# A two-layer LSTM kernel: an own semaphore for the clearing of c, and the two waits of the cell scan written in the other order

## What is computed

```python
def step(carry, xp_t):
    prev_h, prev_c = carry
    h_bar = xp_t + prev_h @ Wh
    i = jax.nn.sigmoid(h_bar[:, 0:Hdim])
    f = jax.nn.sigmoid(h_bar[:, Hdim:2 * Hdim])
    o = jax.nn.sigmoid(h_bar[:, 2 * Hdim:3 * Hdim])
    g = jnp.tanh(h_bar[:, 3 * Hdim:4 * Hdim])
    next_c = f * prev_c + i * g
    next_h = o * jnp.tanh(next_c)
    return ((next_h, next_c), next_h)
```

## Time and profile before

| What | Value |
|---|---|
| median of 3 runs | 485.77 us (484.74 to 487.51) |
| the profiled execution | 481.0 us |
| span of the profiled execution, first to last instruction | 479.0 us |
| mean granted TensorE clock | 0.996 of 2.4 GHz |
| busy: TensorE matmul, VectorE, ScalarE | 97%, 54%, 44% |

### The profile page before, as it was taken

The page is one execution under the profiler, slowest core; times in us unless marked ns, Lnnn a source line. Parts: engine busy times, 40 slices in busy tenths (PEclk is TensorE's granted clock), DMA queues, the critical chain, the costliest instruction groups (busy, mean ns, idle before and its releaser), DMA issues.

```text
span 479.0 us, 17186 instructions
## 1 busy us (share of the span) xinstructions
PE 462.4 (97%) x6440; PEld 349.3 (73%) x6440; DVE 260.7 (54%) x1422; ACT 212.1 (44%) x1092; POOL 17.4 (4%) x29
## 2 busy tenths in 40 slices
PE   7999999999999999999999999999999999999997
PEld 5777666777666777766789877777777777777775
DVE  4545555555555555555545655555555555555554
ACT  2444444544444445444435344444444444444443
POOL 6700000000000000000000000000000000000000
PEclk9989999999999999999999999999999999999999
DMA  5010111110011111010000000000000000000000
GB/s 163 8 19 2 15 16 16 16 16 12 5 16 16 16 16 16 2 15 11 11 13 3 7 19 19 16 16 16 8 8 16 16 16 16 15 1 16 16 16 11
DMA packets 11689, 8.12 MB, mean 17 GB/s; under 512 B 1097, under 2 KB 11129, under 8 KB 11674
## 3 DMA queue, kind: packets, MB, share of 16 engines
q1 hardware_dynamic: 10874, 6.17, 6.5%
q0 software_dynamic: 512, 1.22, 0.9%
q10 hardware_dynamic: 288, 0.52, 0.3%
HBM read 2.87 MB, written 1.05 MB: 8 GB/s over the span
## 4 chain that ended last, share of the span: by engine, by line
PE 88%; DVE 4%; ACT 3%; issue 3%; DMA 1%; DVEq 0%; ACTq 0%
PE fobank L387 20%; PE gibank L377 16%; PE fobank L377 13%; PE bankV L363 5%; PE gibank L352 4%; PE bankY L531 4%; PE gibank L357 4%; PE fobank L352 4%; PE bankU L524 3%; PE fobank L357 3%; DVE cell L750 2%; PE bankV L441 2%; ACT scan L665 2%; PE bankU L459 2%; PE bankU L363 2%
## 5 line engine op out<-in xcount | busy, mean ns | idle before, releaser
L387 PEld LDWEIGHTS fobank<-ring,whf 128*128 128x128 f32 x510 | 76.5, 188 | 94.7 <-DVE ring L753 94.6
L662 ACT ACTIVATE fgate<-fobank 128x16 f32<-128x16 f32 x256 | 46.9, 183 | 164.8 <-PE fobank L387 162.5
L387 PE MATMUL fobank<-ring,whf 128*128 128x16 f32 x510 | 99.5, 270 | 10.4 <-DVE ring L753 0.7
L750 DVE TENSOR_TENSOR_SCAN cell<-scan 128x48 f32<-128x48 f32 x256 | 68.8, 269 | 53.2 <-ACT scan L665 52.8
L746 DVE TENSOR_TENSOR scan<-fgate,cell 128x16 f32<-128x16 f32 x256 | 45.3, 177 | 85.6 <-ACT fgate L662 83.7
L377 PEld LDWEIGHTS gibank<-h_hi,wh_parts 128*128 128x128 bf16 x1536 | 78.8, 110 | 0.0
L753 DVE SCALAR_TENSOR_TENSOR ring<-cell,ogate 128x16 f32<-128x16 f32 x256 | 44.7, 175 | 59.9 <-ACT cell L672 59.9
L377 PE MATMUL gibank<-h_hi,wh_parts 128*128 128x16 f16 x1536 | 75.4, 169 | 0.0
L377 PE MATMUL gibank<-h_lo,wh_parts 128*128 128x16 f16 x1536 | 75.3, 169 | 0.0
L665 ACT ACTIVATE scan<-gibank 128x32 f32<-128x32 f32 x256 | 54.8, 214 | 28.2 <-PE gibank L377 0.2
L377 PE MATMUL fobank<-h_hi,wh_parts 128*128 128x16 f16 x771 | 59.9, 174 | 0.4 <-ACT fgate L662 0.4
(11 more groups left out here) (150 smaller groups left out, 467.1 us busy)
## 6 DMA issues: line engine op xcount, KB each, us to landing
rows_t<-rows SPq DMA_DIRECT2D x16, 128.0 KB
x_rows<-in_x_dram SPq DMA_DIRECT2D x17, 64.0 KB
out_dram<-y_sb SPq DMA_DIRECT2D x16, 64.0 KB
xres<-x2T SPq DMA_DIRECT2D x15, 64.0 KB, 1.9
xin<-x2T SPq DMA_DIRECT2D x14, 64.0 KB, 1.8
w<-in_L_ffn_W_dram POOLq DMA_DIRECT2D x2, 256.0 KB, 3.9
wh<-in_L_cond_Wh_dram ACTq DMA_DIRECT2D x1, 256.0 KB, 2.8
wx<-in_L_cond_Wx_dram ACTq DMA_DIRECT2D x1, 256.0 KB, 3.9
```

The lines of the kernel that those rows point to most:

```text
L387: nc.tensor.matmul(step_out(p, t, GF), whf[layer][:], ring[:, (s - 1) % STEPS, :], start=False, stop=True, skip_group_check=True).then_inc ...
L662: nc.scalar.activation(fgate[:], fobank[p][:, NB * t:NB * t + NB], ACT.Sigmoid).then_inc(f_done[layer], 1)
L750: nc.vector.tensor_tensor_scan(out=c_scan, data0=scan_mul, data1=scan_add, initial=0.0, op0=ALU.mult, op1=ALU.add).then_inc(c_ready[layer], 1)
```

## The change

The clearing of c gets a semaphore of its own, `c_cleared`, and VectorE waits for it once a layer, in `start_h`. The multiplication f*c alone now counts up `fc_done`, so the scan waits for n + 1 and no longer n + 2. And of the two waits ahead of the scan the one for the tanh (`gi_done`) is now written first, the one for f*c second. No arithmetic changes, and no instruction that computes is added or removed.

```diff
+        c_cleared = sem("c_cleared")
...
-            nc.vector.memset(c_psum, 0.0).then_inc(fc_done[layer], 1)
+            nc.vector.memset(c_psum, 0.0).then_inc(c_cleared, 1)
+            nc.vector.wait_ge(c_cleared, layer + 1)
...
                 nc.vector.tensor_tensor(out=fc_slots, in0=fgate[:], in1=c_psum,
                                         op=ALU.mult).then_inc(fc_done[layer], 1)
-                dve.wait_ge(fc_done[layer], n + 2)
                 dve.wait_ge(gi_done[layer], n1)
+                dve.wait_ge(fc_done[layer], n1)
                 nc.vector.tensor_tensor_scan(out=c_scan, data0=scan_mul, data1=scan_add, initial=0.0,
                                              op0=ALU.mult, op1=ALU.add).then_inc(c_ready[layer], 1)
```

## The result

The changed kernel takes 465.45 us (median of 4 runs, 464.69 to 466.24). The kernel before took 486.64 us in the runs beside it (484.74 to 490.51, 4 runs). The ratio is 0.9555, 95% interval 0.9492 to 0.9618: faster by 3.8 to 5.1%. In a later and larger comparison on one chip the same two kernels had medians of 481.26 us (29 runs) and 465.33 us (7 runs), which are 15.9 us apart. Their ratio is 0.9631 (0.9581 to 0.9680), and that is 15.4 to 20.2 us. Medians here are taken over all executions and ratios over those within 1.5% of the fastest of their kernel, so a ratio need not be the quotient of two medians.

What follows compares the result with a forecast made beforehand. A loop of latencies from h back to h was taken to bound the kernel. -16.2 + 0.1 (late multiplications) + 0 to 0.1 (clearing) = -16.1 us, off the median 485.77, gave 469.7 us, range 467.3 to 473.0.

Steps and rivals of the forecast that it cites:

- Which wait is the expensive one: Ahead of the scan, the wait written second becomes an instruction of its own, 21 ns in each of 256 steps.
- The price: At the scan, a carried wait costs 0.033 us, a stand-alone one 0.098; 242 steps x 0.067 = 16.2 us gained.
- The unseen price: Ahead of the scan, the stand-alone wait for VectorE's own multiplication f*c, shown by no row, was taken as 0.098 us.
- TensorE's room: Ahead of TensorE's f-gate weight load, a shortest plain pause of 0.16 us takes up starting 0.067 us earlier.
- the rivals: Nothing changes, 485.8 us (0.07); TensorE's filler limits the gain, 478.5 (0.07); slower, f*c wait last, up to 502.0 (0.06).
- The clearing of c: Its added wait on VectorE costs 0 to 0.1 us; the scan's target falling to n + 1 saves nothing itself.
- The step that failed: The whole-kernel gain of 16.1 us was taken off the runs' median 485.77, not the profiled execution's 481.0, giving 469.7 us.

Runs made afterwards that it cites:

- Run 6: The changed kernel with f*c multiplied once more into a spare tile just ahead of the real multiplication; 478.61 us, ratio 0.9869 to the kernel before.
- run 2: The kernel before with only the order of the two waits swapped, the scan still waiting for n + 2; 486.11 us, ratio 1.0073.
- run 5: The changed kernel with fc_done counted up once more per layer, so the scan waits for n + 2 again; 490.45 us, ratio 1.0141 to the kernel before.
- run 1: The kernel before, unchanged, run again; median 484.55 us over 12 executions, ratio 1.003.
- run 3: The kernel before with only the own semaphore for the clearing of c, the wait order kept; 485.96 us, ratio 1.0045.
- run 12: The changed kernel with 8 instead of 4 matmuls in the first filler; 463.62 us, ratio 0.9617 to the kernel before.
- run 11: The changed kernel, unchanged, run again; 467.13 us, ratio 0.9684 to the kernel before.

## Why the prediction was right in the change and wrong in the time

**Which wait is the expensive one: right.** The wait written second was the instruction of its own, and it lay on the chain. After the change that instruction waits for f*c and has left the chain.

**The price: right.** 0.067 us a step were forecast. The plain step went from 1.77 to 1.70 us, the two stretches that don't depend on the start give 0.069 us, and from the first to the last scan 16.3 us were saved, against 16.1 forecast.

**The unseen price: right.** The stand-alone wait for an own result was taken as 0.098 us. Run 6 measures 0.10 to 0.11.

**TensorE's room: right.** The pauses ahead of the weight load (0.39 to 0.32 us) and the overlap behind line 354 took up the 0.07 us; none of the rivals came.

**The clearing of c: wrong, without a price here.** The forecast said that the target falling from n + 2 to n + 1 "changes a register's value alone", and gave the whole gain to the order. Runs 2 and 5 show that with n + 2 the order brings nothing, since the register operation slips between the waits and takes the wait for the tanh with it. The forecast got the gain right by luck in this point, because both halves were in the change. For the order alone I had expected the whole gain (run 2), and that was wrong by 21 us (486.11 against the changed kernel's 465.33). The register operation already stood in the trace of the kernel before, on the line of the wait written first, and the prediction didn't weigh it:

```profile
L748 DVEq ALU_OP  x233: 40/40/52, 12.2 to 472.6; - x117
```

There it stood ahead of both waits and off the chain: it started 0.01 us behind the start of the multiplication (median). Between the waits, in run 2, it starts 0.03 us behind the end of the tanh and is on the chain.

**The step that failed.** It is this one: "The median of the runs, 485.77, lies 4.8 above that execution; the recurrence is the same in both, so I take the same 16.1 off." The subtraction is sound, the base was not. On the profiled execution it gives 464.9, and the changed kernel measured 465.45; but the range began at 467.3 and left the forecast's own 464.9 out. The 4.8 us were not a constant of the kernel. One program scatters between about 479 and 494 us (run 1), and the kernel before has medians of 481.26, 482.08 and 481.17 us on three chips, not 485.77. Against the larger sample the gain is 481.26 - 465.33 = 15.9 us, and the forecast's 16.1 lies within the interval of the ratio (15.4 to 20.2 us). The range was too narrow at its lower end, because it took the scatter of three runs as the scatter of the kernel: the median alone could move by the 4.8 us that stood in the table.

Where one execution loses against another is shown for profiled ones alone. All profiles of the two loops named above agree to 0.2 us within each of the two later stretches, and differ in the first 32 steps and ahead of them, while TensorE doesn't yet hold its full clock. The clock can also fall later: in run 6's profile it was 0.50 from 305 to 315 us, with 103 matmuls in these 10 us. That the first runs of the kernel before lost their 5 us at the start is inferred; they weren't profiled. It also stays open why all four of them lay above 484.7 us, where only six of the 29 later executions did. It can be chance, or something of that chip and hour.

The profiled spans differ by 14.8 us, 1.5 less than the 16.3 between the scans, and that is the start alone: the first scan started at 12.4 us in the one and at 13.9 in the other, and behind the last scan's start both have 6.0 us.

## What to carry to other kernels

If an instruction of a latency chain needs two waits, write the wait for the result that comes last first, and the other between it and the instruction: in this kernel the first was then carried by the instruction (0.03 us), and the second, which became an instruction of its own (0.10 us), was already over. See to it that both waits compare with a value that already stands in a register, because an operation that works the value out goes between them and takes the first wait away from its instruction; the trace shows this as ALU_OPs in place of EVENT_SEMAPHOREs. And when a profiled execution is 1% below the median of the runs, forecast from both, and let the range span both.

## What the runs showed of the hardware

- The hop from a result to the VectorE instruction that carries its wait is 0.03 us, whether the result is ScalarE's (changed kernel, 199.64 to 199.67) or VectorE's own. A wait on VectorE's sequencer makes it 0.10 us (EVENT_SEMAPHORE, 21 ns; runs 3 and 6), and one carried by a register operation 0.12 us (ALU_OP, 40 ns; runs 2 and 5). The difference of 0.02 is that of the two durations.
- One program of 480 us on one core scatters by over 10 us (run 1: 480.2 to 494.2), and in the two profiles set side by side the difference lies in the time for which TensorE runs at its lower clock at the start. In run 12 it had the full clock from 5 to 18 us while it was busy for 12.31 of 13 us, and the lower one from 18 to 42 us while it was busy for all 24. Why it was lowered there and not in run 11 (23.27 of 24 us busy) stays open.
- A PEclk of 1.00 at the start of a profile need not be the full clock: in run 3 a `keep_warm` matmul took 628 ns on average between 30 and 60 us and 378 ns from 80 to 110 us, with PEclk at 1.00 in both.
